# Band mask of a windowed attention: mask matmuls into PSUM, or a select on GpSimd after the exponential

## The reference, cut to what matters

```python
m = ((j <= i) & (j >= i - 128))          # query i, key j: a band of 129 keys
corr = dot / (norm_i * norm_j + 1e-8) * m
corr = (corr + 1.0) / 2.0
gene_fitness = 1.0 / (denom * sum_inv)   # one number a query and head
weighted = corr * gene_fitness[..., None]
masked = weighted * m + (1.0 - m) * (-1e10)
attn = softmax(masked, axis=-1)          # outside the band: exactly 0
out = attn @ v
```

## Time and profile before

| | us |
|---|---|
| median of three runs | 452.44 |
| the profiled execution | 455.05 |
| its span, first to last instruction | 453.3 |
| PE busy (matmul) | 363.7 |
| DVE busy | 273.4 |
| ACT busy | 229.6 |
| POOL busy | 179.1 |

### The profile page before, as it was taken

One profiled execution on the slowest core, in us unless ns is written; L12 is line 12 of the kernel. 1 busy time (PEld: TensorE's weight loads), 2 busy tenths in 40 slices (PEclk: granted clock), 3 DMA queues, 4 the chain that ended last, 5 costly groups with the idle time before them and its releaser, 6 DMA issues.

```text
span 453.3 us, 9200 instructions
## 1 busy us (share of the span) xinstructions
PE 363.7 (80%) x3121; PEld 226.8 (50%) x3121; DVE 273.4 (60%) x804; ACT 229.6 (51%) x498; POOL 179.1 (40%) x464
## 2 busy tenths in 40 slices
PE   1425887798898989898898989898999989966552
PEld 1214344454656565656465656555656564654242
DVE  0565123335547776768686768575656657888661
ACT  1101555627346657575757475657274647633121
POOL 4743230404224636353645354626152323325241
PEclk9999589959589999899999899989696969998555
DMA  3100000000000101010101010100000000000000
GB/s 88 35 1 23 2 13 0 25 1 23 1 21 5 37 1 37 1 36 4 35 1 36 3 35 1 37 1 25 0 25 2 25 0 25 2 12 13 12 2 25
DMA packets 12407, 7.66 MB, mean 17 GB/s; under 512 B 1027, under 2 KB 12357, under 8 KB 12357
## 3 DMA queue, kind: packets, MB, share of 16 engines
q1 hardware_dynamic: 12356, 7.03, 5.5%
HBM read 4.93 MB, written 2.10 MB: 16 GB/s over the span
## 4 chain that ended last, share of the span: by engine, by line
PE 71%; ACT 11%; issue 7%; DVE 6%; POOL 3%; DMA 0%; SPq 0%; ACTq 0%; POOLq 0%; DVEq 0%
PE OT L689 12%; PE S L668 9%; PE WA L703 8%; PE WD L761 7%; PE S L672 7%; PE WC L709 6%; PE WD L710 5%; PE WB L716 4%; PE WA L787 4%; ACT AT L570 3%; ACT Pm L531 3%; ACT xaT L596 2%; PE WB L828 2%; PE WA L819 2%; ACT y L537 1%
## 5 line engine op out<-in xcount | busy, mean ns | idle before, releaser
L531 ACT ACTIVATE Pm<-S 128x384 f32<-128x384 f32 x256 | 111.9, 492 | 107.9 <-PE S L672 107.2
L668 PE MATMUL S<-mask,ident 128*128 128x384 f16 x256 | 68.9, 354 | 10.0 <-ACT Pm L531 8.4
L461 POOL TENSOR_TENSOR hq<-hm,hs 128x352 f32<-128x352 f32 x32 | 25.2, 788 | 96.9 <-DVE hm L1036 96.8
L689 PE MATMUL OT<-Pm,gv 128*32 128x256 f32 (+1 forms) x1024 | 60.6, 359 | 0.0
L672 PE MATMUL S<-BT,AT 32*128 32x256 f16 (+1 forms) x512 | 45.7, 258 | 0.0
L1012 DVE SCALAR_TENSOR_TENSOR hh<-th,WC 128x352 f32<-128x352 f32 x32 | 16.7, 522 | 44.2 <-ACT th L549 44.2
L689 PEld LDWEIGHTS OT<-Pm,gv 128*32 128x32 f32 x1024 | 28.3, 115 | 22.5 <-issue 7.8
L709 PE MATMUL WC<-wguT,xaT 128*128 128x352 f32 x64 | 29.5, 544 | 11.7 <-ACT xaT L596 7.1
L672 PEld LDWEIGHTS S<-BT,AT 32*128 32x128 f16 x512 | 14.6, 94 | 45.8 <-issue 45.8
L703 PE MATMUL WA<-pick,OTs 128*128 128x36 f32 x256 | 36.7, 306 | 0.0
L668 PEld LDWEIGHTS S<-mask,ident 128*128 128x128 f16 x256 | 19.0, 100 | 34.2 <-issue 16.3
(11 more groups left out here) (142 smaller groups left out, 714.5 us busy)
## 6 DMA issues: line engine op xcount, KB each, us to landing
xT<-x_turned_dram SPq DMA_DIRECT2D x16, 128.0 KB, 2.3
x_res<-x_dram SPq DMA_DIRECT2D x16, 128.0 KB, 2.2
out_dram<-yo SPq DMA_DIRECT2D x16, 128.0 KB, 2.1
wf<-w_down_dram SPq DMA_DIRECT2D x1, 176.0 KB, 2.6
wgv<-wgv_dram SPq DMA_DIRECT2D x1, 128.0 KB, 2.0
wf<-w_gate_dram SPq DMA_DIRECT2D x1, 128.0 KB, 2.2
wf<-w_up_dram SPq DMA_DIRECT2D x1, 128.0 KB, 2.2
woT<-wo_dram SPq DMA_DIRECT2D x1, 64.0 KB
```

What stands on the lines that cost most here:

```text
L461: pool.tensor_tensor(b3(hq[:, k, 0:I]), b3(hm[:, k]), bc(hs[:, k], QB), ALU.mult).then_inc(s_hq, 1)
L531: act.activation(Pm[:, group % PR, hd % 4, :], S[:, (H * x + hd) % 3, 0:SCW], ACT.Exp, scale=1.0 / ZS).then_inc(s_exp, 1)
L668: pe.matmul(S[:, bank, 0:SCW], ident16[:, :], mask16[:, :], start=True, stop=False)
L689: i = pe.matmul(OT[VP * g:VP * (g + 1), col + T - (q1 - q0):col + T], gv[:, x % GVR, kt, H + 4 * c + g, :], Pm[:, (GROUPS * x + c) % PR, g ...
```

## The change

The mask matmuls go. PE writes the scores of all keys straight into the bank, and ACT takes exp of all of them. A new POOL function `band(x, c)` waits for the four exponentials of a group and then runs three `affine_select` instructions over Pm in place, one for each 128-column block of all four heads (128 partitions x 4 x 128, f32), which write zero outside the band. `values` waits for `s_band` in place of `s_exp`. In iteration t POOL runs band(t-1, 3) first of all, band(t, 0) behind the cast to B16, band(t, 1) behind the second hn, and band(t, 2) last.

```diff
@@ GpSimd, setup
-            pool.memset(mask16[:, :], 0.0).then_inc(c_pool, 1)
...
-            for m, fill in ((win16, 0.0), (mask16, MASKED)):
+            for m, fill in ((win16, 0.0),):
...
+            def band(x, c):
+
+                if not live(x):
+                    return
+                pool.wait_ge(s_exp, H * x + 4 * c + 4)
+                e = Pm[:, (GROUPS * x + c) % PR].rearrange("p g (b q) -> p g b q", q=P)
+                for k, sign in ((0, 1), (1, -1), (2, 1)):
+                    pool.affine_select(out=e[:, :, k, :], in_=e[:, :, k, :], compare_op=ALU.is_ge, fill=0.0, base=0,
+                                       pattern=[[0, 4], [sign, P]], channel_multiplier=-sign).then_inc(s_band, 1)
@@ GpSimd, the loop
             for t in range(FIRST, LAST + 1):
 
+                band(t - 1, 3)
                 if live(t + 2):
                     newton(t + 2, (0, 1))
...
                     pool.tensor_copy(B16[:, :, 0:3:2, :], twice(Bf)).then_inc(s_Bhi, 1)
+                band(t, 0)
                 if live(t - 3):
                     h_over_scale(t - 3, 0)
...
                 if live(t - 3):
                     h_over_scale(t - 3, 1)
+                band(t, 1)
+                if live(t - 3):
                     h_times_scale(t - 3, 0)
...
                 if live(t - 3):
                     h_times_scale(t - 3, 1)
+                band(t, 2)
@@ TensorE, scores
-                for hd, bank in pair:
-                    pe.matmul(S[:, bank, 0:SCW], ident16[:, :], mask16[:, :], start=True, stop=False)
...
-                                      BT[r:r + 32, x % 2, c, T - (q1 - q0):T], start=False, stop=(kt == 1))
+                                      BT[r:r + 32, x % 2, c, T - (q1 - q0):T], start=True, stop=True)
@@ TensorE, values
-                pe.wait_ge(s_exp, H * x + 4 * c + 4)
+                pe.wait_ge(s_band, 3 * (GROUPS * x + c) + 3)
```

More of the change, by code:

```diff
@@ L92, in layer @@
         ones16 = sb("ones16", [P, P], BF16)
-        mask16 = sb("mask16", [P, SCW], F16)
         win16 = sb("win16", [P, SCW], F16)
@@ L215, in layer @@
         s_exp = sem("s_exp")
+        s_band = sem("s_band")
         s_pv = sem("s_pv")
@@ L407, in _ @@
             pool.memset(win16[:, :], 1.0).then_inc(c_pool, 1)
-            pool.memset(mask16[:, :], 0.0).then_inc(c_pool, 1)
             pool.memset(mhalf[:, :], -0.5).then_inc(c_pool, 1)
-            pool.wait_ge(c_pool, 18)
-            for m, fill in ((win16, 0.0), (mask16, MASKED)):
+            pool.wait_ge(c_pool, 16)
+            for m, fill in ((win16, 0.0),):
                 for k, sign in ((0, 1), (1, -1), (2, 1)):
@@ L722, in _ @@
                     pe.wait_ge(c_dve, 15)
-                    pe.wait_ge(c_pool, 28)
+                    pe.wait_ge(c_pool, 24)
                 scores(t, 0)
```

## The result

The changed kernel has a median of 487.26 us over four runs (483.59 to 489.42), the kernel before 452.21 us over four. The ratio is 1.075, 95% interval [1.069, 1.081]: slower, by 35 us. The prediction said slower, 475 us, range 455 to 498. In the profiled execution it is 485.35 us with a span of 483.5, where before it was 455.05 and 453.3.

What follows compares the result with a forecast made beforehand. PE was taken to set the pace; after the change the ring through hm would, at 24.4 us a period against 22.37. Over 13 iterations +26 us, less 3.5 in iterations 0 to 2: median 475 us, range 455 to 498.

Steps and rivals of the forecast that it cites:

- The ring through hm: Loop of POOL's newton and cast B, DVE's B, PE's turn, DVE's rounding, POOL again: 18.64 us before, 22.06 after.
- The sum of one period: Ring 22.06 us, DVE's B held up 0.5, DVE's rounding held up 0.8, clock 1.0: 24.4 us against 22.37.
- +26 was forecast: Iterations 3 to 15, where the ring is closed: +2.0 us a period, +26 us over 13 iterations.
- The price of a select: On POOL, a select taken to cost what the cast of 512 does: 0.57 us from one to the next.
- The dear select of the rivals: Rival: selects on POOL cost up to 1.0 us start to start, 509 us, half of that way 492; chance 0.12.
- In iterations 0 to 2 ... half of the 2.6 us may show: First three iterations, no hm yet, PE sets the pace: -1.2 us each, -3.5 us together.
- What the change removes ... 2.6 us: On PE, the mask matmuls: the chain's 9%, 41 us in 16 batches, 2.6 us a period.
- PE alone would then go at about 18.7 us: PE without the mask matmuls, in an undisturbed period: about 18.7 us, before 21.23.
- band(t, 0) ... Hidden, band(t, 1) ... Hidden: On POOL, 1.7 us of selects each, hidden in the 1.58 us wait for hr and the 5.30 us wait for hm.
- 1.3 us: POOL and DVE delaying each other: 0.5 us at DVE's B, 0.8 us at DVE's rounding of x behind orec.
- The clock: PE's clock falls behind a longer gap ahead of the turn of B: 1.0 us a period, bounds 0.3 and 1.6.
- the rule of two SBUF inputs: A DVE instruction with two SBUF inputs and a GpSimd instruction reading SBUF exclude each other; the later one waits.

Runs made afterwards that it cites:

- e5_neither_fill: Kernel before without mask matmuls or selects (mask left out of the computation), plus 12 filler matmuls ahead of the turn of B; 431.23 us, ratio 0.953.
- both cures at once: Changed kernel with only groups 0 and 1 banded, masks for 2 and 3, band 0 held until B is made, 10 filler matmuls; ratio 0.997, about 450 us.

## Why the prediction was right, and where it was not

- **Direction, and the loop in which it lies: right.** The ring through hm closed as described, with the selects ahead of the newton steps and the seed no longer waited for. Band 3 twice cost 28 us for 25 expected. PE's wait for DVE's B (3.56 us), the longer B (1.11), the half clock in each period, and POOL's 302 us of busy time are there as forecast.
- **The sum of one period.** Forecast 22.06 + 0.5 + 0.8 + 1.0 = 24.4. Measured from 212.08 to 236.48, 24.40, of: newton to cast 5.41 (5.60), cast to the end of B 1.75 (1.33 + 0.5), until PE starts 0.15 (0.06), B's turn to orec 3.79 (2.42 + 1.0), orec to hq 5.92 (5.38 + 0.8), hq to hq 3.10, second hq 0.74, six selects 3.54 (3.42). Other periods run to 25.8, and the mean of the table's eleven is 24.65. That this one meets 24.4 to the hundredth is luck: newton, B and the rounding came out shorter than the forecast, the clock longer. From orec of iteration 3 to that of 16 it took 310.4 us for 283.8 before, +26.6 where +26 was forecast:

```profile
L1158 DVE RECIPROCAL orec<-WA x14: 357/357/358, 122.9 to 433.3; 128x32 f32<-128x32 f32 x14
```
```profile
L1146 DVE RECIPROCAL orec<-WA x14: 357/358/358, 118.7 to 402.5; 128x32 f32<-128x32 f32 x14
```

  The first is of the changed kernel, the second of before. This agreement is in part luck too. Up to the orec of iteration 15 it is +22.4, 1.9 us a period for the forecast 2.0, and the last period alone adds 4.1.

- **The price of a select: right.** The cast's row was a good stand-in, 0.63 us for 0.61, and the six in the ring take 0.59 us from one to the next for the 0.57 charged. The dear select of the rivals (0.77 us and more) was not found. Beside DVE's instructions a select is longer, up to 1.13 us:

```profile
L432 POOL TENSOR_SCALAR_AFFINE_SELECT Pm<-Pm x192: 628/635/1127, 48.2 to 426.4; 128x512 f32<-128x512 f32 x192
```

- **The step that failed: "In iterations 0 to 2 ... half of the 2.6 us may show", -3.5 us.** It was +4.2 (orec of iteration 3 at 122.9 for 118.7), 7.7 us off. The clock stood at half for longer there. The same stretch, of the changed kernel and of before:

```profile
59.20:80.20 21.00, 17.63 (x133) 11.33 (x137) 6.15 (x12) 9.32 (x20) 11.89 (x26) 0.50 0.00 1
```
```profile
59.20:80.20 21.00, 16.59 (x192) 8.96 (x190) 6.87 (x20) 12.51 (x28) 4.30 (x14) 1.00 0.03 7
```

  The kernel before was back at full clock from 59 us on. The changed one stood at half until 80 us and, but for 3.4 us, until 104. With neither masks nor selects the clock stands at half for most of the same time (44 to 78 us, but for 3.4 us), and the orec of iteration 3 comes at 121.6: the missing matmuls alone are enough for 2.9 of the 4.2 us. With fillers in the changed kernel that orec comes at 116.9, ahead of before. That the selects have no part in it is not shown: with masks and bands together the orec comes at 125.0, in the one profile there is.

- **"What the change removes ... 2.6 us", "PE alone would then go at about 18.7 us": wrong.** With neither masks nor selects, and the clock held, a period is 20.7 us for the undisturbed 21.2. The gain is 0.5 us. PE's order is bound by a second ring (B, values back, xm, genes, seed, newton, B) that I had left out of the sum; its row of before was the 1.85 us wait for the seed, which I read as slack of the ring through hm alone. In `e5_neither_fill` PE waits for it in each period:

```profile
207.49 0.41 PE L797 MATMUL WC<-identf,xm 128*128 128x128 f32 x2 [0.64 <-DVE xm L1095]
```

  With bands 0 and 1 alone it is this ring that closes (POOL waits for the seed again). How its 20 us divide between the clock and the collisions was not measured apart, only both cures at once.
- **"band(t, 0) ... Hidden, band(t, 1) ... Hidden": wrong as to DVE.** They lie in POOL's waits, but beside DVE's busy stretches, for which the sum did charge 1.3 us. Bands 0 and 1 alone, with half of the mask matmuls gone, cost 20 us.
- **The clock: right in kind, too small.** 1.0 us was charged in 13 periods and 1.4 were found in the one above. In the mean of eleven, 4.29 us from the end of B to orec less 0.15 to get PE going and 2.42 at full clock leave 1.7, past the upper bound of 1.6. Its share over the whole kernel is larger still, since even the kernel before loses 19 us to it. Removing the mask matmuls alone gives 464.5, which is 10 us above before; the selects add 23 more, to 487.3.
- **A reading on the way.** Of the two pairs that were held against the rule of two SBUF inputs, only DVE's hm has two. L1026, 0.75 us for 0.34 beside hq, reads one tensor. The slowing was read rightly, but that row does not bear out a rule about two inputs, and the selects slow such instructions as well (xu above).
- The rest of the 12 us between 475 and 487 is spread among executions: the profiled ones lie 30.3 apart, the medians 35, and nothing here explains those last 5.

## What to carry to other kernels

When an engine keeps the pace and its work is taken away in front of a wait, ask first whether the wait only grows. Here half of the 256 matmuls stood ahead of such a wait. Removing them all was worth 7 us over 13 periods with the clock held, and made the kernel 10 us slower without. A gap of TensorE in a periodic loop is worth a few filler matmuls before anything is moved: 7 of them in a 1.28 us gap gave 4.3%, more than any change of the mask. And work put into another engine's idle time is hidden only if it does not slow a third engine that is busy then: here GpSimd's selects filled GpSimd's waits and made DVE's instructions longer, in a ring that had 0.5 us to spare.

## What was not expected of the hardware

- Removing work made the kernel slower: 454.32 to 464.48 us, with the granted clock down from 0.88 to 0.78 in the mean. Adding 105 matmuls of no use to the kernel before (7 in each of 15 iterations) made it 19 us faster.
- The clock fell behind a gap of 1.28 us in some periods only, and behind gaps of 2.4 and 3.6 us in nearly all. It then stayed at half for 7 us or more (rows above), where one such stretch of before had 3.2 us. Why the gap of 1.28 us brings a fall in some periods and not in others stays open.
- A select on GpSimd and a DVE instruction with two SBUF inputs delay each other: 1.11 us for 0.69 (B, A) and 0.85 for 0.42 (xn) on DVE, up to 1.13 us for 0.63 on GpSimd. A TENSOR_SCALAR that reads one tensor is slowed by a select as well: xu 0.60 us for 0.29, and in the changed kernel even small ones, hs (128x44) 0.61 for 0.18 and the seed (128x32) 0.55 for 0.18. The RECIPROCAL orec kept its 0.36 us throughout.
